# A recurrence on one core: the TensorE loop holds one pair of steps instead of two, with one PSUM bank for each gate

## What is computed

```python
Xz = einsum('btc,hc->tbh', X, Wxz) + bxz        # the same for r and h; all 512 steps at once
def step(H, xs):                                # 512 steps, one after the other
    xz, xr, xh = xs
    Z = sigmoid(xz + H @ Whz.T + bhz)
    R = sigmoid(xr + H @ Whr.T + bhr)
    H_tilda = tanh(xh + (R * H) @ Whh.T + bhh)
    H_new = Z * H + (1 - Z) * H_tilda
    return H_new, H_new @ Whq.T + bhq
x = x + transpose(Ys, (1, 0, 2))
```

## Time and profile before

| | us |
|---|---|
| median of 3 runs | 2276.43 |
| lowest, highest | 2246.28, 2291.57 |
| the profiled execution | 2232.23 |
| its span (first to last instruction) | 2230.3 |
| PE busy (matmuls) | 2132.6 |
| DVE, ACT, POOL busy | 1589.5, 1226.0, 888.9 |

### The profile page before, as it was taken

One profiled execution on the slowest core, in us unless ns is written; L12 is line 12 of the kernel. 1 busy time (PEld: TensorE's weight loads), 2 busy tenths in 40 slices (PEclk: granted clock), 3 DMA queues, 4 the chain that ended last, 5 costly groups with the idle time before them and its releaser, 6 DMA issues.

```text
span 2230.3 us, 206497 instructions
## 1 busy us (share of the span) xinstructions
PE 2132.6 (96%) x88464; PEld 2054.4 (92%) x88464; DVE 1589.5 (71%) x9106; ACT 1226.0 (55%) x5994; POOL 888.9 (40%) x1830
## 2 busy tenths in 40 slices
PE   8899999999999999999999999999999999999997
PEld 7799999999999999999999999999999999999997
DVE  4777777777777777777777777777777777777776
ACT  2455555555555555555555555555555555555554
POOL 3344344444344443444443444434444434444331
PEclk9999999999999999999999999999999999999999
DMA  3000000000000100000000000000000000000000
GB/s 153 16 28 17 26 24 21 26 24 21 26 24 19 28 17 26 24 21 26 24 21 26 23 19 28 16 26 24 21 26 24 21 26 24 19 28 16 26 20 22
DMA packets 84278, 58.27 MB, mean 26 GB/s; under 512 B 9490, under 2 KB 75410, under 8 KB 83474
## 3 DMA queue, kind: packets, MB, share of 16 engines
q1 hardware_dynamic: 84240, 57.81, 8.7%
q10 hardware_dynamic: 4, 0.02, 0.0%
HBM read 41.01 MB, written 16.78 MB: 26 GB/s over the span
## 4 chain that ended last, share of the span: by engine, by line
PE 95%; issue 4%; DMA 1%; DVE 1%; ACT 0%; SPq 0%; DVEq 0%
PE u_bank L620 42%; PE v_bank L620 20%; PE y_bank L555 9%; PE d_bank L523 7%; PE b_bank L523 6%; PE a_bank L523 6%; PE c_bank L523 3%; DMA w_all<-in_w_x 0%; PE b_bank L540 0%; PE a_bank L540 0%; PE u_bank L540 0%; DVE pre_t L980 0%; PE c_bank L540 0%; DMA y_io<-in_x_res 0%; DVE scanned L1082 0%
## 5 line engine op out<-in xcount | busy, mean ns | idle before, releaser
L980 DVE STREAM_TRANSPOSE pre_t<-u_bank 128x32 f32<-128x32 f32 (+1 forms) x3072 | 455.1, 199 | 278.2 <-PE u_bank L620 241.4
L620 PE MATMUL u_bank<-wh,scanned 128*16 128x128 f32 (+1 forms) x16384 | 548.5, 273 | 82.8 <-issue 74.9
L317 POOL TENSOR_TENSOR x_parts<-z_of 128x96 f32<-128x96 f32 x744 | 341.6, 459 | 556.7 <-DVE h_sums L1000 243.1
L620 PE MATMUL u_bank<-wh,reset_state 128*16 128x128 f32 (+1 forms) x16384 | 556.4, 273 | 3.7 <-DVE reset_state L1133 2.5
L620 PE MATMUL v_bank<-wh,scanned 128*16 128x128 f32 (+1 forms) x16384 | 548.1, 273 | 0.0
L620 PEld LDWEIGHTS u_bank<-wh,scanned 128*16 128x16 f32 (+1 forms) x16384 | 428.5, 103 | 112.4 <-issue 103.7
L620 PEld LDWEIGHTS v_bank<-wh,scanned 128*16 128x16 f32 (+1 forms) x16384 | 460.9, 104 | 0.3 <-issue 0.2
L620 PEld LDWEIGHTS u_bank<-wh,reset_state 128*16 128x16 f32 (+1 forms) x16384 | 428.4, 103 | 18.2 <-DVE reset_state L1133 14.0
L968 ACT ACTIVATE scan_on<-pre_t 128x16 f32<-128x16 f32 (+1 forms) x1536 | 237.8, 219 | 288.8 <-DVE pre_t L980 288.8
L942 ACT ACTIVATE r_gate<-pre_t 128x16 f32<-128x16 f32 (+1 forms) x1536 | 234.5, 215 | 255.4 <-DVE pre_t L980 247.9
L317 POOL TENSOR_TENSOR z_of<-z_of 128x96 f32<-128x96 f32 x558 | 255.9, 459 | 275.5 <-DVE reset_state L1133 173.1
(11 more groups left out here) (141 smaller groups left out, 2848.9 us busy)
## 6 DMA issues: line engine op xcount, KB each, us to landing
y_io<-in_x_res SPq DMA_DIRECT2D x256, 64.0 KB, 2.0
out<-y_io SPq DMA_DIRECT2D x256, 64.0 KB, 1.6
x_all<-in_x_t SPq DMA_DIRECT2D x62, 256.0 KB, 2.6
w_all<-in_w_x SPq DMA_DIRECT2D x2, 1536.0 KB, 7.6
wh<-in_w_hr SPq DMA_DIRECT2D x1, 1024.0 KB, 10.7
wh<-in_w_hz SPq DMA_DIRECT2D x1, 1024.0 KB, 14.2
wh<-in_w_hh SPq DMA_DIRECT2D x1, 1024.0 KB, 16.2
wq<-in_w_q SPq DMA_DIRECT2D x1, 1024.0 KB, 6.4
```

What stands on the lines that cost most here:

```text
L317: nc.gpsimd.tensor_tensor(*of, ALU.add).then_inc(made, 1)
L620: mm = nc.tensor.matmul(gate_rows(g, par, slice(Q * j, Q * j + rows)), of, wh[g][:, m, P * j:P * (j + 1)], start=False, stop=(m == G - 1), ...
L980: nc.vector.transpose(flat(pre_t[g][:, a:b]), gate_part(g, par, a, b)).then_inc(done, 1)
```

## The change

PE's loop body becomes one pair of steps. Three nested loops run around it: k (1 to turns - 2), `later` (0, 1) and `odd` (0, 1). `odd` says which pair of the half turn it is, and both the output products and the x products of a step are chosen by a branch on it, in which the old branches on `later` stand. The loops have neither `head_slot` nor `hint_back_edge`, so the head lies where the code before it ends, which is at the end of a fetch block. Three half turns are written out at the end.

R, Z and H get one PSUM bank each, used by every pair, and three copies of x parts (`put`) instead of two. `scanned` is single; ACT copies the states that the output products and sums read later into `kept_a` and `kept_b`. DVE waits for those copies before it overwrites states. At the start, one more part of the x products is kept in `x_first`, and three banks are filled with biases instead of two. Several waits in the x products move behind the first blocks or to ACT. Cut to its core:

```diff
-        scanned = sb("scanned", [P, 2, G, 3 * B, 2])
-        states = scanned[:, :, :, :, 1]
+        scanned = sb("scanned", [P, G, 3 * B, 2])
+        states = scanned[:, :, :, 1]
+        kept_a = sb("kept_a", [P, G, Q])
+        kept_b = sb("kept_b", [P, half, Q])
-        u_bank = [bank("u_bank0"), bank("u_bank1")]
-        v_bank = bank("v_bank")
+        gate_bank = [bank("r_bank"), bank("z_bank"), bank("h_bank")]
...
+            def pair(q, between, gap):
+                begin = isinstance(q, int) and q == 0
+                for s in range(2):
+                    t = 2 * q + s
+                    if s == 0 and not begin:
+                        pe.wait_ge(gate_put[R], q)
+                    recur(R, t, s)
...
+                    if s == 0 and not begin:
+                        pe.wait_ge(gate_put[Z], q)
+                    recur(Z, t, s)
...
+                    between(s)
+                    if s == 0 and not begin:
+                        pe.wait_ge(gate_put[H], q)
+                    recur(H, t, s)
+                    gap(s)
...
-            def batch_gap(c, n, later):
+            def batch_gap(c, k, later):
                 with pe.If(later):
-                    with pe.If_lt(pe.to_reg(n), turns - 2):
-                        batch_goes_on(c, n)
+                    batch_goes_on(c, k)
                 with pe.Else():
                     if c == 0:
-                        with pe.If(n):
-                            batch_ends(n)
-                    with pe.If_lt(pe.to_reg(n), turns - 2):
-                        batch_begins(c, n)
+                        with pe.If(k - 1):
+                            batch_ends(k - 1)
+                    batch_begins(c, k)
...
+            def pair_of_loop(k, later, odd):
+                i = 2 * k - 1 + later
+                def between(s):
+                    with pe.If(odd):
+                        outputs_between(2 + s, i)
+                    with pe.Else():
+                        outputs_between(s, i)
+                def gap(s):
+                    with pe.If(odd):
+                        batch_gap(2 + s, k, later)
+                        outputs_gap(2 + s, i)
+                    with pe.Else():
+                        batch_gap(s, k, later)
+                        outputs_gap(s, i)
+                pair(4 * k - 2 + 2 * later + odd, between, gap)
...
-            half_turn(0, 0, plain_gap, first=True)
-            with nc.Fori(0, turns - 1, engines=[mybir.EngineType.PE], head_slot={mybir.EngineType.PE: 0}, hint_back_edge=True) as n:
-                with nc.Fori(0, 2, engines=[mybir.EngineType.PE], hint_back_edge=True) as later:
-                    half_turn(2 * n + 1 + later, 8 * n + 4 + 4 * later, lambda c: batch_gap(c, n, later))
-            half_turn(2 * turns - 1, 8 * turns - 4, lambda c: None, end=True)
+            half_turn(0, plain_gap, first=True)
+            with pe.Fori(1, turns - 1) as k:
+                with pe.Fori(0, 2) as later:
+                    with pe.Fori(0, 2) as odd:
+                        pair_of_loop(k, later, odd)
+            half_turn(2 * turns - 3, last_gap)
+            half_turn(2 * turns - 2, lambda c: None)
+            half_turn(2 * turns - 1, lambda c: None, end=True)
...
+            def put(g, values):
+                nc.scalar.copy(gate_bank[g][:, 0:P], values[:, X_AT[g]:X_AT[g] + P]).then_inc(gate_put[g], 1)
+
+            def keep_a(i):
+                if not isinstance(i, int) or i > 0:
+                    act.wait_ge(ys4_ready, i + 1)
+                    act.wait_ge(q2_done, i)
+                for h in range(N):
+                    act.wait_ge(state_ready[h], 4 * i + 3)
+                nc.scalar.copy(kept_a[:], states[:, :, B:3 * B]).then_inc(kept_a_ready, 1)
+
+            def keep_b(i):
+                if not isinstance(i, int) or i > 0:
+                    act.wait_ge(q34_done, i)
+                nc.scalar.copy(kept_b[:], states[:, half:G, B:3 * B]).then_inc(kept_b_ready, 1)
...
-                    if s8 in (1, 3, 5) and (not first or s8 > 1):
-                        put_u(1 - par, x_part(p + 1, n))
-                    elif s8 == 7 and not last:
-                        put_u(0, x_part(0, n + 1))
-                    elif s8 == 2 and ends:
+                    if s == 1 and not (last and s8 == 7):
+                        put(R, x_part((p + 1) % 4, n + (p + 1) // 4))
+                    if c == 0:
+                        keep_b(i)
+                    elif c == 2:
+                        keep_a(i)
+                    if s8 == 2 and ends:
                         start_b_d(n - 1)
...
                     nc.scalar.activation(z_gate[:], pre_t[Z][:, :, mine], ACT.Sigmoid).then_inc(z_ready, 1)
+                    if s == 1 and not (last and s8 == 7):
+                        put(Z, x_part((p + 1) % 4, n + (p + 1) // 4))
...
+                    if c == 0:
+                        dve.wait_ge(kept_b_ready, i + 1)
+                        if not begin:
+                            dve.wait_ge(ys4_ready, i + 1)
+                    elif c == 2:
+                        dve.wait_ge(kept_a_ready, i + 1)
                     for h in range(N):
-                        renew(t, h, par, s)
+                        renew(t, h, s)
```

More of the change, by code:

```diff
@@ L354, in combine_x2, with wait_put @@
                 elif op == 6:
-                    wait_put(v_put[1], 2 * (k + 1) + 1)
+                    wait_put(4 * (k + 1) + 3)
                 combine(op, made_x2, lambda b: z[:, :, PLACE[b], :], lambda i, l: part(i, l, None, 1), k)
-            def wait_put(put, count):
-                pool.wait_ge(put, count)
+            def wait_put(pair):
+                pool.wait_ge(gate_put[H], pair)
             def after_state(t):
@@ L557, in y_product, with of_a, of_b @@
                 return mm
-            def state(par, part):
-                return lambda m: states[:, par, part * half + m, B:3 * B]
+            def of_a(part):
+                return lambda m: kept_a[:, part * half + m, :]
+            def of_b(m):
+                return kept_b[:, m, :]
             def state_sum(n):
@@ new lines, in outputs_between @@
+            def outputs_between(c, i, first=False, end=False):
+                if c == 0:
+                    pe.wait_ge(ys2_ready, i + 1)
+                    q6()
+                elif c == 1:
+                    pe.wait_ge(q16_copied, i + 1)
+                    q7()
+                elif c == 2:
+                    pe.wait_ge(kept_b_ready, i + 1)
+                    if end:
+                        pe.wait_ge(yv_b_put, i)
+                    else:
+                        pe.wait_ge(q_filled, i + 1)
+                    q4()
+                elif not end:
+                    pe.wait_ge(yv_a_put, i + 1)
+                    q2()
@@ L659, in half_turn, with outputs_gap @@
+            def outputs_gap(c, i, first=False, end=False):
+                if c == 1:
+                    if first:
                         pe.wait_ge(yt_ready[0], 2)
-                        q5()
-                    elif c == 2:
-                        pe.wait_ge(ys4_ready, i + 1)
+                    q5()
+                elif c == 2:
+                    pe.wait_ge(ys4_ready, i + 1)
+                    if first:
                         pe.wait_ge(wq_loaded, 16)
-                        q3()
-                        if not end:
-                            q1()
-                    elif c == 3 and end:
-                        pe.wait_ge(y_filled, 2)
-                        project_y(0).then_inc(y_projected, 1)
+                    q3()
+                    if not end:
+                        pe.wait_ge(kept_a_ready, i + 1)
+                        q1()
+                elif c == 3 and end:
+                    pe.wait_ge(y_filled, 2)
+                    pe.wait_ge(kept_a_ready, i + 1)
+                    project_y(0).then_inc(y_projected, 1)
@@ L671, in plain_gap, with half_turn @@
+            def half_turn(i, x_gap, **at):
+                for p in range(2):
+                    def gap(s):
+                        x_gap(2 * p + s)
+                        outputs_gap(2 * p + s, i, **at)
+                    pair(2 * i + p, lambda s: outputs_between(2 * p + s, i, **at), gap)
             def plain_gap(c):
@@ L896, in turn @@
                     end = last and odd == 1
-                    if s == 0 and (not first or p >= 2):
-                        put_v(par, x_part(p, n))
+                    if s == 0 and (not first or p >= 1):
+                        put(H, x_part(p, n))
                     if first:
-                        for q in {0: (2, 3), 1: (4,), 2: (5,), 3: (6,), 4: (7,)}.get(s8, ()):
+                        for q in {0: (1, 2), 1: (3, 4), 2: (5,), 3: (6,), 4: (7,)}.get(s8, ()):
                             keep_plain(q)
@@ L989, in state_sums @@
             def state_sums(i):
-                h_a0, h_a1, h_b0, h_b1 = (states[:, par, part * half:(part + 1) * half, B:3 * B]
```

(4 more changed lines are left out.)

219 lines of the change are left out of this document (95 added, 124 removed).

## The result

The changed kernel takes 2354.16 us, the median of 4 runs (2353.47 to 2355.51). The kernel before, on the same chip, has 2284.0 us (4 runs, 2246.28 to 2338.37). The ratio is 1.0411, with a 95% interval of 1.0293 to 1.053: slower. Ratios leave out slow runs, more than 1.5% above a kernel's shortest; of the kernel before two are left, 2246.28 and 2276.43 us.

What follows compares the result with a forecast made beforehand. PE was taken as the bound, 96% busy, idling at loop edges. Edges 3.34 plus inner branches 0.65 less removed 1.63 gave 2.36 us a turn, times 62 = 146 us, on 2276: 2422 us, range 2330 to 2515.

Steps and rivals of the forecast that it cites:

- The offset of 44 us: Gap between the earlier kernel's median, 2276.4 us, and its profiled execution, 2232.2; unexplained by the trace, kept in the forecast.
- Edges: Four loop back edges a turn on PE: odd 0.53 us idle twice, middle 0.92, outer 1.36; sum 3.34.
- Registers: Register operations computing the pair number from three loop variables at each edge: 0.4 us, between 0.33 and twice that.
- The half of a second jump: Part of the outer edge's records: 0.12 us for half of a second jump.
- The lead behind q5: How far PE's sequencer runs ahead at the odd edge, behind q5's 64-column products: 0.25 us.
- Inside the body: New branches on `odd` in each `between` and `gap`: 0.65 us a turn, between 0.1 and 1.0.
- Removed, 1.63: Both old edges, 1.55 us, and the third step's add for n + 1, at most 0.1, saved each turn.
- ACT, 0: Extra ACT copies of x parts and states add 0 to a turn; 0.1 a turn, 6 us, for the range.
- Start and end: Extra kept part and third bank at the start, three written-out half turns at the end: 0, within 5 us.
- Blocks: PE's new body takes 5.7 instruction blocks, eight stay resident, none loads in the loop; reloading rival had chance 0.09.
- Branch prices: PE's branches record to record: taken 0.28 us, not taken 0.13, jump 0.25; the skill's 51 and 108 ns would give 2340.
- What would show it: Signs: "issue" idle before R more than doubles from 75.8 us, about 248 places, turn near 36.4 us, no loop block loads.

Runs made afterwards that it cites:

- the variant without the head's place: The kernel before with its hints but without head_slot on the outer loop: span 2429.0 us.
- the layout alone: Also "the layout with half turns": changed kernel's banks, copies and waits with PE's old half-turn loop, head_slot and hints: median 2221.43 us, ratio 0.9951 to kernel before.
- the variant with four records more: Changed kernel with four increments of an unused semaphore at the end of each pair's body, ahead of the back edge: span 2479.9 us.

## Why the prediction was right, and where its terms were off

The direction, the mechanism and the range were right: PE's sequencer pays for the added edges. The forecast on the profiled execution was 2378 us and that execution took 2354.01. Its terms:

**The offset of 44 us: wrong, and it is most of the miss.** The forecast added it because the median of before lay above its profiled execution. Those 44 us belong to the scatter of the kernel before; the changed kernel's runs lie within 2 us of its profiled one. A sum made on a profiled execution should not have been given an offset that no row explains. Without it the forecast is 24 us off instead of 68. What the scatter is, no profile shows. An estimate from the variant without the head's place: its 13 reloads took 199 us and 0.021 of the mean granted clock (0.998 to 0.977), so 15 us and 0.0016 each. Two spans of the kernel before on one chip, 2226.1 us at 1.000 and 2257.2 at 0.996, lie apart as two such reloads would put them, and 44 us would be three. A run of that kind would have to be profiled to settle it.

**Edges: 3.34 forecast, 2.88 measured.** The records are those foreseen; three terms were mis-sized. Registers were taken at 0.4 and take 0.30, a little under the row that was the lower bound, at four edges: 0.4 us. The half of a second jump, 0.12 on the outer edge, does not exist: both jumps go to one place. The lead behind q5 was taken at 0.25; the add begins at 1007.4 and R at 1008.07, 0.66 us, less 0.34 idle is 0.32, so 0.07 twice. These make some 0.66 where the forecast was 0.46 too high; the difference is mostly two moves at the outer edge that were not counted (four where two stood in the sum, 0.18).

**Inside the body: 0.65 forecast, 0.57 with the add for n + 1 taken off, and 0.73 measured, but for another reason.** With the head in slot 0 a turn is 35.50 us. Against the layout with half turns (33.97) that is 1.53 more, of which the edges are 2.84 - 1.53 = 1.31, so 0.2 is left for the added branches. The other 0.6 goes with the place of the head. That the number came near is chance: branches were priced too high, and the place was not priced at all. What it is about the place that costs time stays open.

**Removed, 1.63.** The two old edges are gone as stated. The add for n + 1 was taken at 0.08; outside its edges the layout alone has 33.97 - 1.53 = 32.44 us where the kernel before has 32.51, which fits but is not told apart from other causes.

**ACT, 0: right.** The layout alone has a turn of 33.97 us, not longer than the kernel before (34.06).

**Start and end, 0 within 5 us: nearly right,** about -6.

**Blocks: right.** None is loaded in the loop. That the margin is real is shown from the other side: the body of 7.2 blocks does reload, as soon as either the hint or the place is missing.

**Branch prices.** Taken 200 to 209 ns, not taken 63 to 75, jumps 163 to 169. The prices of the forecast came from loops with hints, where each is a little longer. The rule of the Trainium skill weighed in the prediction (Advanced Engine Details and Errata, section Control Flow Timing) would have given 2340 with the offset and 2296 without; 2354 was measured, and the sum by the records gives 2378 without the offset. That rule of the Trainium skill is too low for taken branches and jumps, and too high for branches that are not taken.

**What would show it.** "issue" ahead of R was to more than double, in about 248 places. It rose by half, in 199. The gaps are there, but the odd ones, 0.34 and 0.37 us, are partly under what the view puts down as idle; only the variant with four records more shows all 248. The forecast took 0.2 us off each gap for the view, which with the measured gaps gives (2.88 - 0.8) x 62 = 129 us; the rest is that it counted every gap as seen. The turn was to be near 36.4 us and is 36.12.

## What to carry to other kernels

Price a loop edge as the sum of its sequencer records, from record to record, less the lead that the products ahead of it give, and then ask where in the body that lead is longest: here the same edges cost 1.6 us a turn less when moved behind 128-column products, half of it by the lead and half by records that no longer stood in the edge. Then look behind the edge as well: what has used up the lead there can show up as idle time two products later. Nested loops with a small body multiply the edges; derive loop variables only as far as one or two cheap operations do it, and check that the body stays resident before dropping a hint or a head's place. Keep the forecast on the profiled execution, and don't add an offset that no row explains.

## What the runs showed of the hardware that was not expected

**A stall of 5 us on PE costs more than itself.** In the kernel before without hints, PE idles for 5.1 us at an outer edge, and then runs at half clock. Stretches around it (length, busy time of PE, PEld, DVE, ACT, POOL, granted clock, DMA share, GB/s):

```profile
1490.00:1500.00 10.00, 10.00 (x452) 9.94 (x442) 7.33 (x46) 6.09 (x31) 3.35 (x8) 1.00 0.12 34
1500.00:1505.30 5.30, 0.20 (x12) 0.05 (x8) 0.96 (x6) 0.48 (x1) 0.77 (x2) 0.73 0.08 18
1505.30:1508.90 3.60, 3.60 (x76) 2.97 (x80) 0.88 (x6) 0.76 (x4) 0.39 (x1) 0.50 0.02 5
```

The timeline of PE in the last of these stretches:

```profile
1505.25 1.91 PE L620 MATMUL u_bank<-wh,scanned 128*16 128x128 f32 x32 [5.10 <-issue]
1506.93 1.94 PE L620 MATMUL v_bank<-wh,scanned 128*16 128x128 f32 x32
```

From R at 1505.25 to Z at 1506.93 is 1.68 us for a gate set that takes 0.88 at full clock: the granted clock is 0.50, which is the level of 1.2 GHz, after an idle of 5.1 us. This is part of why a reload costs 14.4 us a turn. The edges of the changed kernel, 1.3 us at most, leave the clock at its full level.

**Others.** With hints on the loops PE's branches take 3 to 20 ns longer, and a hint costs 0.09 us itself. The place of the same code in the instruction blocks moved a turn by 0.6 us. A semaphore increment takes PE's sequencer 0.15 us. PE's sequencer is 0.47 to 0.63 us ahead of PE behind a gate set of 128 columns, 0.43 behind x blocks of 96 and 0.32 behind an output product of 64.
